# Hand-overs between the stages of an eight-stage Flamingo block: fewer returning transfers, other setup order, and small moves in the routing

## The chip, the core and the metric

One core of a Trainium2 chip runs the whole program in one launch. The metric is the device time in microseconds, median of repeated runs. TensorE multiplies and transposes (a transpose is a matmul with the identity), VectorE, ScalarE and GpSimd compute, and SP (SyncE) issues most transfers. Every stage is a block of its own: at its end all five engines meet, and GpSimd collects them and lets them go.

## The reference

`x` is 16 batches of 112 tokens of width 256, float32. Four layers follow, each a gated attention over a context of 375 tokens and a gated feed-forward net:

```python
x = x + tanh(g_xattn[l]) * xattn_l(layernorm(x), ctx)
x = x + tanh(g_ffn[l])   * ffn_l(layernorm(x))
# attention: softmax(q k^T * scale + mask) v, then an output projection and bias
#   layer 0: 8 heads of 32, then a spline (KAN) layer;   layer 1: 16 heads of 64, key mask
#   layer 2: 16 heads of 16, rotary q and k;             layer 3: 16 heads of 16, score mask
# nets: 0: soft decision tree;  1: 8 experts, dense, top-2 gates
#   2: 8 experts, rms norm, top-2 softmax, silu(x W1a + b) * (x W1b + b) W2
#   3: 9 experts, sigmoid scores, top-2, silu(x w1) * (x w3) w2
```

## The kernel before

`x_all` [112 tokens, 16 batches, 256] stays in SBUF between stages. An attention stage is a software pipeline over batches b = -1 .. 16: at step t the engines work at batch t's probabilities and prepare batch t+1 (norm, transposes, q, k, v). Four groups of four heads (i = 0 .. 3) make up a step; `CYCLES` says which projection TensorE does between the transposes of a group. Each engine's program is written out in order, and semaphores tie them:

- VectorE: `begin_norm` (bn_stats, bn_aggr, variance + eps; line 1011 ff.), then GpSimd's `power` (line 532) gives 1/sqrt, then VectorE's `norm_apply` (line 1022) writes `xn`. TensorE turns `xn` (line 670), ScalarE copies it, and q is projected. In layers 2 and 3 q is then split in two halves (`halve_q`, line 1080); in layer 2 GpSimd first rotates k (lines 545 to 551) and q (559 to 567). The scores are at line 749, their row maximum at 1092 or 1098, the exponentials (ScalarE) at 869, the transposes of the probabilities at 762, their copies at 1118 (VectorE) and 876 (ScalarE), the product with v at 780.
- In the group loop VectorE begins the norm of batch t+2 in group i = 2 and applies that of t+1 in group 0.
- Setup at the start of a stage, on VectorE: clear `v` (layers 2 and 3, line 989) or the probabilities (layer 1, line 1007), turn the mask into summands (992), prepare the value bias (1000), which TensorE multiplies by the output weights (804) and VectorE adds to the bias row (1002, 1004). Only then comes `begin_norm(0)`. GpSimd first clears the semaphores of the stage before (`clear_spent`, line 127).

The routed stages (layers 2 and 3) normalise all rows (`kept`, 1993), turn them in eight pairs (1798), score them (1807), and choose two experts per token. A table in four rounds of eight columns then puts each token into a slot of 35 or 36 tiles of 128: per round VectorE marks the tile (`spots`, 2084), multiplies by the token's number (2087) and marks the slot (2089), GpSimd multiplies the marks by the token's share (1712), and TensorE sums (1842). The tiles follow: GpSimd gathers rows (1719), TensorE turns them (1856), up projections (1867), down (1878), VectorE scales (2123), GpSimd adds the rows to `sums` in HBM (1731). SP loads the weights of each tile, double buffered (1758 to 1765). At the end of layer 2's stage SP waits for the last add and brings x back, one transfer per batch (1778), all on one semaphore; the attention of layer 3 waits for batch b with `16 * (b + 1)`.

## Time and profile before

| | |
|---|---|
| median of 3 runs | 2823.93 us (2821.07 to 2824.85) |
| profiled execution | 2821.64 us, span 2819.8 us, mean granted clock 0.975 |
| busy TensorE / VectorE / ScalarE / GpSimd | 94% / 54% / 46% / 22% |
| HBM traffic | 250.08 MB read, 18.48 MB written |

The stages in the span, and TensorE's busy time in each:

| stage | us from the span's start | length | TensorE busy |
|---|---|---|---|
| layer 0 attention | 11 to 422 | 411 | 371.6 |
| layer 0 tree | 422 to 471 | 49 | 39.1 |
| layer 1 attention | 471 to 1205 | 734 | 720.6 |
| layer 1 experts, dense | 1205 to 1333 | 128 | 118.9 |
| layer 2 attention | 1333 to 1685 | 352 | 328.6 |
| layer 2 experts, routed | 1685 to 2125 | 440 | 410.6 |
| layer 3 attention | 2125 to 2469.7 | 344.7 | 325.4 |
| layer 3 experts, routed | 2469.7 to 2820 | 350.3 | 322.5 |

How to read it: what a stage's TensorE time leaves is idle time of the engine that does most. It is not spread evenly: it sits at the starts of the stages, in the routing, and in small repeated waits. A row of the timeline gives the start, the duration, the engine and line, what is written from what, and in brackets how long the engine stood idle before it and which engine ended that.

### The profile page before, as it was taken

Reading aid. Unit: us, or ns where it says so; the run is one execution under the profiler, and the core shown is the slowest. Engines: PE = TensorE matmul, PEld = TensorE weight load, DVE = VectorE, ACT = ScalarE, POOL = GpSimd, SP = SyncE. Lnnn points to the kernel's source line nnn. Section 1 sums busy time; section 2 is a strip of 40 time slices with the busy share of each in tenths; the row PEclk is TensorE's granted clock in tenths of the full one; section 3 lists DMA queues with packets and bytes.
Section 4 is the critical chain, followed back from the end, with each engine's and each line's share of the span. In section 5 each row is a group of like instructions: output and inputs, shape, how many; then the busy total and the mean of one; then the engine's idle time right before and its main releaser. Section 6 shows DMA issues by size and latency. Waiting matters only on the chain. (4 is left out here: it accounts for less than half of the span.)

```text
span 2819.8 us, 56614 instructions
## 1 busy us (share of the span) xinstructions
PE 2637.1 (94%) x19850; PEld 1993.0 (71%) x19850; DVE 1532.3 (54%) x4127; ACT 1285.7 (46%) x3546; POOL 622.8 (22%) x577
## 2 busy tenths in 40 slices
PE   6999978999999999889899988999997999979998
PEld 4777755666666666655666666999995777758887
DVE  4667757555555555446677774232325777752222
ACT  4777733343343434321676752333335777622221
POOL 1666551000000000010444331222220000023232
PEclk9999989999999999999999998999998999989999
DMA  4000002000000000010000016999981000059897
GB/s 123 18 18 18 12 10 99 13 13 7 13 7 13 8 12 7 1 34 3 18 24 18 18 34 219 327 330 328 329 282 50 18 22 20 7 193 310 306 305 239
DMA packets 92163, 269.52 MB, mean 96 GB/s; under 512 B 25276, under 2 KB 51124, under 8 KB 77588
## 3 DMA queue, kind: packets, MB, share of 16 engines
q1 hardware_dynamic: 74708, 244.48, 25.0%
q0 software_dynamic: 13632, 18.62, 3.1%
q10 hardware_dynamic: 3616, 3.67, 0.4%
q8 instruction: 129, 2.11, 0.3%
q14 instruction: 78, 0.64, 0.1%
HBM read 250.08 MB, written 18.48 MB: 95 GB/s over the span
## 5 line engine op out<-in xcount | busy, mean ns | idle before, releaser
L762 PEld LDWEIGHTS a_full_ps<-ident,a_probs 112*125 112x125 f32 x2688 | 368.1, 190 | 130.5 <-issue 65.2
L1867 PEld LDWEIGHTS m_banks<-m_x_inT,m_w 128*128 128x128 f32 x3824 | 437.0, 193 | 15.4 <-issue 13.6
L1867 PE MATMUL m_banks<-m_x_inT,m_w 128*128 128x128 f32 x3824 | 444.1, 277 | 1.4 <-ACT m_x_inT L1931 0.9
L762 PE MATMUL a_full_ps<-ident,a_probs 112*125 112x112 f32 x2688 | 418.3, 282 | 19.1 <-ACT a_v L838 7.0
L869 ACT ACTIVATE a_probs<-a_masked,a_negmax 112x375 f32<-112x375 f32 x512 | 305.5, 598 | 280.2 <-DVE a_negmax L1092 280.1
L1118 DVE COPY a_pT<-a_full_ps 125x448 f32<-125x448 f32 x448 | 276.5, 620 | 254.6 <-PE a_full_ps L762 251.4
L663 PE MATMUL a_full_ps<-attention_room 128*125 128x256 f32 (+1 forms) x960 | 329.8, 472 | 11.4 <-ACT a_qT L861 3.9
L655 PE MATMUL a_full_ps<-attention_room 128*128 128x375 f32 x896 | 322.4, 488 | 1.4 <-ACT a_q_raw L857 0.7
L1092 DVE CUSTOM_DVE_ANT_0 a_masked<-a_sc_ps,a_mask_add 112x375 f32<-112x375 f32 x512 | 249.6, 544 | 29.9 <-PE a_sc_ps L749 29.9
L780 PEld LDWEIGHTS a_o_ps<-a_pT,a_v 125*32 125x32 f32 (+1 forms) x5376 | 164.4, 118 | 134.2 <-issue 106.1
L869 ACT ACTIVATE a_probs<-a_sc_ps,a_negmax 112x375 f32<-112x375 f32 x384 | 216.6, 576 | 92.8 <-DVE a_negmax L1098 92.8
L749 PE MATMUL a_sc_ps<-a_kT,a_qT 32*112 32x375 f32 (+1 forms) x1792 | 241.2, 512 | 6.7 <-ACT a_probs L869 3.3
L1878 PE MATMUL m_banks<-m_w,m_hid 128*128 128x256 f32 x992 | 232.9, 383 | 0.0
L663 PEld LDWEIGHTS a_full_ps<-attention_room 128*125 128x125 f32 x960 | 166.0, 188 | 92.3 <-issue 65.4
L780 PE MATMUL a_o_ps<-a_pT,a_v 125*32 125x112 f32 (+1 forms) x5376 | 216.4, 266 | 14.4 <-DVE a_pT L1118 10.8
L1098 DVE TENSOR_REDUCE a_negmax<-a_sc_ps 112x2 f32<-112x750 f32 x192 | 171.3, 934 | 94.8 <-PE a_sc_ps L749 94.8
L1731 POOL DMA_INDIRECT p_sums<-m_y_out,m_put x71 | 112.6, 1586 | 479.6 <-DVE m_y_out L2123 285.7
L1945 ACT ACTIVATE m_silu<-m_banks,m_b 128x128 f32<-128x128 f32 x280 | 102.8, 367 | 240.3 <-PE m_banks L1867 232.7
L655 PEld LDWEIGHTS a_full_ps<-attention_room 128*128 128x128 f32 x896 | 159.9, 194 | 70.9 <-issue 3.4
L1878 PEld LDWEIGHTS m_banks<-m_w,m_hid 128*128 128x128 f32 x992 | 180.0, 190 | 31.9 <-issue 11.9
L532 POOL TENSOR_TENSOR a_rstd<-a_rstd,minus_half 112x1 f32<-112x1 f32 x64 | 35.2, 549 | 734.0 <-DVE a_rstd L1015 726.9
L2109 DVE SCALAR_TENSOR_TENSOR m_hid<-m_banks,m_b,m_silu 128x128 f32<-128x128 f32 x280 | 98.1, 351 | 163.2 <-ACT m_silu L1945 163.2
(261 smaller groups left out, 3449.0 us busy)
## 6 DMA issues: line engine op xcount, KB each, us to landing
m_w<-in_L2f_w SPq DMA_DIRECT2D x105, 1024.0 KB, 6.7
m_w<-in_L3f_w SPq DMA_DIRECT2D x72, 768.0 KB, 4.6
attention_room<-in_ctxT SPq DMA_DIRECT2D x64, 375.0 KB, 3.1
m_w<-in_L3f_w SPq DMA_DIRECT2D x36, 640.0 KB, 5.4
m_b<-in_L2f_b SPq DMA_DIRECT2D x35, 128.0 KB, 8.0
p_sums<-x_all ACTq DMA_DIRECT2D x2, 1792.0 KB, 8.8
p_rows<-m_kept SPq DMA_DIRECT2D x16, 224.0 KB, 3.5
attention_room<-in_L0x_spline_wT SPq DMA_DIRECT2D x1, 2048.0 KB, 10.9
```

Of the source, the lines that this page charges most:

```text
L655: mm = pe.matmul(use_ps[:, 0:SK], wk[:, c, u[1] * P:(u[1] + 1) * P], ctxT[:, par, c, :], start=(c == 0), stop=(c == DC - 1))
L663: mm = pe.matmul(use_ps[0:KT, 0:v_width], ctxT[:, par, c, k * KT:(k + 1) * KT], wv[:, c, part * v_width:(part + 1) * v_width], start=(c == ...
L749: pe.matmul(sc_ps[:, a, 0:SK], lhs, kT[r:r + k, par, c, :], start=True, stop=True)\
L762: mm = pe.transpose(full_ps[0:KT, bank_of["turn", i, k], (j % 4) * S:(j % 4 + 1) * S], probs[:, i % 2, a, t * KT:(t + 1) * KT], ident[0:S, ...
L780: mm = pe.matmul(o_ps[a % WIDE * VW:(a % WIDE + 1) * VW, block * S:(block + 1) * S], v[:, par, t, head(i, a), :], pT[:, i % 2, KC * a + t, :],
L869: act.activation(probs[:, i % 2, a, 0:SK], src, ACT.Exp, bias=negmax[:, m:m + 1], scale=-1.0 if mask else 1.0, accum_out=rowsum[:, par, n: ...
L1092: dve.tensor_tensor_reduce(out=masked[:, i % 2, a, :], in0=sc_ps[:, a, 0:SK], in1=bias, scale=-1.0, scalar=FLT_MAX, op0=ALU.add, op1=ALU.m ...
L1098: dve.tensor_reduce(negmax[:, m:m + 2], sc_ps[:, 2 * a:2 * a + 2, 0:SK], AX.X, ALU.max, negate=True).then_inc(s_max.sem, 1)
L1118: dve.tensor_copy(pT[:, i % 2, 4 * k:4 * (k + 1), :], full_ps[0:KT, bank_of["turn", i, k], 0:4 * S] .rearrange("p (j s) -> p j s", j=4)).t ...
L1731: pool.indirect_dma_start(plan.sums, bass.IndirectOffsetOnAxis(plan.put[:, t:t + 1], 0), y_out[:, t % 2, :], None, compute_op=ALU.add).the ...
L1867: mm = pe.matmul(ab_ps[:, (par * FC + f) % RING, i * SLOTS:(i + 1) * SLOTS], w[:, par, c, f * P:(f + 1) * P], x_inT[:, c, :], start=(c == ...
L1878: mm = pe.matmul(y_ps[:, par, 0:D], hid[parts[f], f, :], w2[parts[f], par, f, :], start=(f == 0), stop=(f == FC - 1))
```

## The change

Borders. (1) x comes back in five transfers (batches 0, 1, 2-3, 4-7, 8-15), each on a semaphore of its own, instead of sixteen. (2) GpSimd no longer waits for the last added rows itself; SP still does.

Attention setup. (3) `begin_norm(0)` is the first work of VectorE but for a small copy. (4) `v` is cleared by GpSimd, one half (1536 elements per partition) in step -1 and one in step 0, each behind or ahead of other work of that engine; ScalarE waits for the half that it writes. (5) The value bias, the score mask, and in layer 1 the bias scaling and the clearing of the probabilities move into step -1. (6) The semaphore clears move to the end of GpSimd's step -1, behind the bias add of batch 0.

Layer 3's loop. (7) The norm of batch t+1 is begun in group 0 of step t (before: t+2 in group 2) and applied in the same group, behind one copy; GpSimd's power leads its step.

Routing. (8) The first two groups of rows are normalised ahead of the memsets and the gate scale, and TensorE turns five pairs before it waits for the routing weights. (9) The multiplication by the shares goes from GpSimd (4 instructions of 8 columns) to ScalarE (32 of one column). (10) SP waits for the first two gathers before it issues the second tile's weights.

```diff
@@ attention_stage @@
+    normed = 1 if layer == 3 else 2
 # gpsimd
-                core.clear_spent(pool)
+                if kan:
+                    core.clear_spent(pool)
                 def body(t, par):
+                    if layer == 3 and exists(t + 1):
+                        power(t + 1)
+                    if hd == 16 and isinstance(t, int) and t < 1:
+                        pool.memset(v[:, t + 1], 0.0).then_inc(s_zero.sem, 1)
                     if rope and exists(t + 1):
                         rope_add(t + 1, 1 - par, 0)
-                    if exists(t + 1):
-                        if isinstance(t, int) and t == -1:
-                            pool.wait_ge(s_bo.sem, 3 if late else 1)
+                    if exists(t) and exists(t + 1):
                         add_bias(t + 1)
 ...
-                    if exists(t + 2):
+                    if exists(t + 2) and layer != 3:
                         power(t + 2)
 ...
+                    if isinstance(t, int) and t == -1:
+                        pool.wait_ge(s_bo.sem, 3 if late else 1)
+                        add_bias(0)
+                        core.clear_spent(pool)
 # scalar, copy of v
-                            act.wait_ge(s_zero.sem, 1)
+                            act.wait_ge(s_zero.sem, b + 1)
 # vector
-                if hd == 16:
-                    dve.memset(v[:], 0.0).then_inc(s_zero.sem, 1)
 ...
-                        if divided and i == 0 and exists(t + 1):
+                        if layer == 2 and i == 0 and exists(t + 1):
                             norm_apply(t + 1)
 ...
-                        if i == 2 and exists(t + 2):
-                            begin_norm(t + 2)
+                        if i == (0 if layer == 3 else 2) and exists(t + normed):
+                            begin_norm(t + normed)
 ...
-                            if not divided:
+                            if layer != 2:
                                 norm_apply(t + 1)
 ...
+                        if divided and isinstance(t, int) and t == -1 and i == 1:
+                            value_bias()
@@ moe_stage @@
+BACK = (range(0, 1), range(1, 2), range(2, 4), range(4, 8), range(8, B))
 # gpsimd
-                for p in range(C // SPOTS):
-                    c = slice(p * SPOTS, (p + 1) * SPOTS)
-                    pool.wait_ge(s_in_tile.sem, p + 1)
-                    pool.tensor_tensor(in_tile[:, c, SHARES:], spots[:, c], share ... ALU.mult)
-                pool.wait_ge(s_put.sem, 16 * T)
 # sync
                 def body(t, par):
+                    if isinstance(t, int) and t == 1:
+                        for i in range(2):
+                            sp.wait_ge(s_x[i].sem, 16)
                     load(t, par)
 ...
-                    for b in range(B):
-                        sp.dma_start(x_all[:, b, :], plan.sums[b * S:(b + 1) * S, :]).then_inc(s_back.sem, 16)
+                    for group, back in zip(BACK, s_back):
+                        sp.dma_start(x_all[:, group.start:group.stop, :], plan.sums[...]).then_inc(back.sem, 16)
 # tensor
+                for p in range(5):
+                    turn_pair(p)
                 pe.wait_ge(s_w.sem, 16 * len(loads))
 # scalar
+                for c in range(C):
+                    if c % SPOTS == 0:
+                        act.wait_ge(s_in_tile.sem, c // SPOTS + 1)
+                    ins = act.activation(in_tile[:, c, SHARES:], spots[:, c], ACT.Copy, scale=share[...][:, c:c + 1])
+                    if c % SPOTS == SPOTS - 1:
+                        ins.then_inc(s_shares.sem, 1)
```

VectorE at the start of layer 3's attention, before (a_bvb is the value bias spread over the tokens, a_qT the halved q):

```order
L989 MEMSET a_v 125x3072
L992 TENSOR_SCALAR a_mask_add<-a_mask_in 112x375
L1000 COPY a_bvb<-attention_room 128x224
L1002 TENSOR_TENSOR attention_room<-a_o_ps,attention_room 112x256
L1004 TENSOR_SCALAR attention_room<-attention_room,gates 112x256
L1011 BN_STATS a_stats<-x_all 112x6
L1013 BN_AGGR a_mv<-a_stats 112x2
L1015 TENSOR_SCALAR a_rstd<-a_mv 112x1
L1022 TENSOR_SCALAR a_xn<-x_all,a_mv,a_rstd 112x256
L1080 TENSOR_SCALAR a_qT<-a_qfull,attention_room 128x224 x2
```

and of the change (line numbers are the changed kernel's):

```order
L1007 COPY a_bvb<-attention_room 128x224
L1017 BN_STATS a_stats<-x_all 112x6
L1019 BN_AGGR a_mv<-a_stats 112x2
L1021 TENSOR_SCALAR a_rstd<-a_mv 112x1
L1028 TENSOR_SCALAR a_xn<-x_all,a_mv,a_rstd 112x256
L1012 TENSOR_TENSOR attention_room<-a_o_ps,attention_room 112x256
L1014 TENSOR_SCALAR attention_room<-attention_room,gates 112x256
L1291 TENSOR_SCALAR a_mask_add<-a_mask_in 112x375
L1086 TENSOR_SCALAR a_qT<-a_qfull,attention_room 128x224 x2
```

The clearing is gone from VectorE, and the bias row and the mask stand between xn and the halves of q. Layer 2's start is the same without the mask, and with the shuffles of k and q ahead of the bias row.

VectorE in one step of layer 3's loop, before: first group 2, then, after the row maxima, group 0 of the next step:

```order
L1080 TENSOR_SCALAR a_qT<-a_qfull,attention_room 128x224 x2
L1011 BN_STATS a_stats<-x_all 112x6
L1013 BN_AGGR a_mv<-a_stats 112x2
L1015 TENSOR_SCALAR a_rstd<-a_mv 112x1
L1118 COPY a_pT<-a_full_ps 125x448 x2
...
L1022 TENSOR_SCALAR a_xn<-x_all,a_mv,a_rstd 112x256
L1127 TENSOR_TENSOR a_oT<-a_o_ps,a_rt 128x224
L1118 COPY a_pT<-a_full_ps 125x448 x2
```

and of the change, group 0 and then group 2 of one step:

```order
L1133 TENSOR_TENSOR a_oT<-a_o_ps,a_rt 128x224
L1017 BN_STATS a_stats<-x_all 112x6
L1019 BN_AGGR a_mv<-a_stats 112x2
L1021 TENSOR_SCALAR a_rstd<-a_mv 112x1
L1124 COPY a_pT<-a_full_ps 125x448
L1028 TENSOR_SCALAR a_xn<-x_all,a_mv,a_rstd 112x256
L1124 COPY a_pT<-a_full_ps 125x448
...
L1086 TENSOR_SCALAR a_qT<-a_qfull,attention_room 128x224 x2
L1124 COPY a_pT<-a_full_ps 125x448 x2
```

The three statistics instructions left the place between q's halves and the two copies, and xn stands behind them and one copy of group 0.

GpSimd at the start of layer 3's attention, before (L127 clears a semaphore, L532 is the power, L538 the bias add):

```order
L127 ISA x45
L532 TENSOR_TENSOR a_rstd<-a_rstd,minus_half 112x1
L538 TENSOR_TENSOR x_all<-x_all,attention_room 112x256
L532 TENSOR_TENSOR a_rstd<-a_rstd,minus_half 112x1
L538 TENSOR_TENSOR x_all<-x_all,attention_room 112x256
```

and of the change:

```order
L535 TENSOR_TENSOR a_rstd<-a_rstd,minus_half 112x1
L619 MEMSET a_v 125x1536
L541 TENSOR_TENSOR x_all<-x_all,attention_room 112x256
L127 ISA x45
L535 TENSOR_TENSOR a_rstd<-a_rstd,minus_half 112x1
L619 MEMSET a_v 125x1536
L541 TENSOR_TENSOR x_all<-x_all,attention_room 112x256
```

The clears went behind the first bias add, and each power is followed by half of the clearing of v in the first two rounds.

## Rows read from the trace of the kernel before

**Rows 1.** Stretches: us, busy PE, PEld, DVE, ACT, POOL, PEclk, DMA, GB/s

```profile
1685.00:2125.00 440.00, 410.56 (x3028) 384.57 (x3028) 145.42 (x446) 141.40 (x398) 97.30 (x78) 0.96 0.89 299
```

**Rows 2.** Timeline, TensorE, layer 1's attention: start us, us, instruction, idle before

```profile
482.08 1.53 PE L655 MATMUL a_full_ps<-attention_room 128*128 128x375 f32 x4 [0.59 <-DVE a_v L1048]
```

**Rows 3.** Timeline, start of layer 2's attention, VectorE, ScalarE, GpSimd

```profile
1332.06 2.62 DVE L989 MEMSET a_v<- 125x3072 f32 x1 [0.99 <-PEq L2182]
...
1339.33 0.41 DVE L1022 TENSOR_SCALAR a_xn<-x_all,a_mv,a_rstd 112x256 f32<-112x256 f32 x1 [0.66 <-POOL a_rstd L532]
...
1341.90 0.60 ACT L857 ACTIVATE a_q_raw<-a_full_ps,attention_room 128x112 f32<-128x112 f32 x2 [1.30 <-PE a_full_ps L678]
...
1343.08 0.64 POOL L538 TENSOR_TENSOR x_all<-x_all,attention_room 112x256 f32<-112x256 f32 x1
...
1344.97 0.66 POOL L567 TENSOR_TENSOR a_qfull<-a_qrot_a,a_qrot_b 128x224 f32<-128x224 f32 x1 [0.18 <-POOL a_qrot_b L562]
```

**Rows 4.** Line 1993's instructions, ns min/median/max, and GpSimd's memset, routing of layer 2

```profile
L1993 DVE TENSOR_SCALAR m_kept<-x_all,m_mv,m_rstd x16: 394/402/1162, 1687.7 to 1693.3; 112x256 f32<-112x256 f32 x16
...
1689.17 0.89 POOL L1707 MEMSET attention_room<- 112x928 f32 x1
```

**Rows 5.** Timeline, table of layer 2, second round: VectorE, GpSimd; ScalarE later

```profile
1712.09 0.44 DVE L2084 TENSOR_TENSOR attention_room<-route_room,m_high 112x280 f32<-112x280 f32 x1
...
1712.67 0.95 DVE L2087 TENSOR_TENSOR attention_room<-attention_room,route_room 112x280 f32<-112x280 f32 x1
...
1713.54 1.21 DVE L2089 TENSOR_TENSOR net_room<-route_room,m_low 112x1024 f32<-112x1024 f32 x1
...
1712.66 0.65 POOL L1712 TENSOR_TENSOR attention_room<-attention_room,m_share 112x280 f32<-112x280 f32 x1 [1.94 <-DVEq L2086]
...
1722.72 0.20 ACT L1924 ACTIVATE m_part<-m_banks 128x35 f32<-128x35 f32 x1 [19.55 <-PE m_banks L1847]
```

**Rows 6.** Timeline, first gather and tiles, GpSimd, TensorE, layers 2 and 3

```profile
1723.81 1.24 POOL L1719 DMA_INDIRECT m_x_in<-p_rows,m_take  x1 [5.31 <-DVE m_take L2095]
...
1730.23 0.69 PE L1856 MATMUL m_banks<-ident,m_x_in 128*128 128x128 f32 x2 [3.93 <-DMA m_x_in<-p_rows,m_take]
...
1731.78 9.28 PE L1867 MATMUL m_banks<-m_x_inT,m_w 128*128 128x128 f32 x64 [0.87 <-ACT m_x_inT L1931]
...
1744.57 7.31 PE L1867 MATMUL m_banks<-m_x_inT,m_w 128*128 128x128 f32 x64
...
2511.30 1.10 POOL L1719 DMA_INDIRECT m_x_in<-p_rows,m_take  x1 [5.28 <-DVE m_take L2095]
...
2514.20 0.44 PE L1856 MATMUL m_banks<-ident,m_x_in 128*128 128x128 f32 x2 [0.36 <-DMA m_x_in<-p_rows,m_take]
```

**Rows 7.** Timeline, border to layer 3's attention: SP, VectorE, TensorE

```profile
2116.82 7.38 SPq L1778 DMA_DIRECT2D x_all<-p_sums  x16
...
2125.31 2.62 DVE L989 MEMSET a_v<- 125x3072 f32 x1 [12.45 <-PEq L1702]
...
2128.59 2.02 PE L804 MATMUL a_o_ps<-attention_room,a_bvb 128*112 128x256 f32 x4 [16.25 <-DVE a_bvb L1000]
...
2137.30 0.90 PE L749 MATMUL a_sc_ps<-a_kT,a_qT 32*112 32x375 f32 x8
```

**Rows 8.** Waits (total, times, longest us) and timeline inside layer 3's attention

```profile
PE a_o_ps L780 <- DVE a_pT L1118: 8.1, 14, 0.6
...
2317.94 0.42 DVE L1011 BATCH_NORM_STATS2 a_stats<-x_all 112x6 f32<-112x256 f32 x1
...
2318.96 0.55 POOL L532 TENSOR_TENSOR a_rstd<-a_rstd,minus_half 112x1 f32<-112x1 f32 x1 [10.49 <-DVE a_rstd L1015]
...
2327.56 0.08 DVE L1092 DVE_READ_ACCUMULATOR2_ANT a_negmax<- 112x1 f32 x1
...
2329.69 0.35 PE L670 MATMUL a_full_ps<-ident,a_xn 112*128 112x112 f32 x2
```

**Rows 9.** Timeline, GpSimd, start of the tree stage

```profile
421.81 3.27 POOL L109 TENSOR_TENSOR f_rstd<-f_rstd,minus_half 112x2 f32<-112x2 f32 x2 [12.42 <-issue]
```

62 lines of the change are left out of this document (32 added, 30 removed).

## The prediction, made before the changed kernel ran

> **What bounds the kernel now.** I read the busy table first, then the stretches by stage, then each stage border in order of time. The busy table gives TensorE 94% of the span, so only TensorE's idle time can be won. In the stretches that idle time lies at the borders, in the routing ahead of the expert tiles (29.4 us idle in the 440 of layer 2's expert stage, [rows 1]), and as one short stall per batch in the last attention stage [rows 8]. Inside the expert tiles TensorE stands back to back, though the DMA engines are 89% busy there [rows 1]; that matters for a rival. So each border is a chain, and a step's price is how much earlier the first matmul behind it can start.
>
> **Part 1, layer 1's attention start.** VectorE scaled the bias and cleared the probabilities before its first statistics and copies. TensorE stood idle 0.59 us ahead of the first key projection, for VectorE's last value copy [rows 2]. The clearing is not gone: it now stands behind the copies of the first group of heads, so it delays the next two copies instead. I take that idle, **0.6**, as won; bounds nothing (the clearing still in the way) and twice that (an earlier wait of the same kind goes too).
>
> **Part 2, layer 2's attention start.** Before, VectorE cleared the values (2.62 us), TensorE then did the value bias, and only then came the first statistics. From their start to xn's is 1.6 us (0.85 on VectorE, 0.24 to the power, 0.55 for it [rows 8]), so they began near 1337.7, 5.7 us after the clearing began at 1332.06 [rows 3]. Now only a small bias copy leads, so they begin near 1332.3. GpSimd's power then ends near 1333.9, but GpSimd next clears half of the values: 1536 elements at the rate of its 928 in 0.89 us [rows 4] is 1.5 us, to 1335.3. VectorE's xn works on the same SBUF side by side with it. In the routing the same kind of VectorE instruction took up to 1162 ns against 402 beside GpSimd's work [rows 4], so I let xn end behind the memset, at 1335.7, against 1339.74: 4.1 us earlier. From xn to q_raw took 2.76 us [rows 3], so q_raw is there at 1338.4. GpSimd's q rotation then began only at 1343.68, 1.2 behind q_raw, as the key rotation and the bias add (0.64) stood ahead; now the add stands at the end. I get qfull at 1340.5 instead of 1345.63: **5.1 us**. Bounds 4 (the key rotation late by a whole memset) and 6 (xn not held up).
> By the Trainium skill, page "SBUF — State Buffer", section on its ports ("Reading the diagram"), GpSimd and a VectorE operation in a two-port mode take one shared port pair as an exclusive lock for the whole instruction. That speaks against moving the memset to GpSimd right behind the power: by it xn waits out the memset, which is the 1.1 us I already counted from the rows; without it the start would gain 6.
>
> **The semaphore clears** also move to the end of GpSimd's first round. In the tree stage 41 of them stand ahead of the first power, which began at 421.81 with GpSimd waiting for nothing that the trace shows [rows 9], 3 us into the stage: some 70 ns each. Layer 2 clears 24 (1.7 us) and layer 3 45 (3.2 us), each before work that has 5 us of GpSimd idle ahead of it in the trace (layer 2) or starts later still (layer 3). Cost nothing; uncovered at most 3.
>
> **Part 3, routing, head (both expert stages).** The first two groups of rows are normalised before the memsets and the gate scale (about 0.9 us in layer 2, 0.6 in layer 3). But the fifth pair, which TensorE turns before the first scores, comes from the third group, and that is where it was. **0.2 and 0**, bounds 0 and 0.9.
>
> **Part 4, routing, table (both).** Each of four rounds on VectorE has three instructions; the second one, of the same 280 elements as the first, takes 0.95 us against 0.44, and starts within 0.01 us of GpSimd's multiply (0.65) [rows 5]. The change gives that multiply to ScalarE. Then the second should cost about 0.45: 4 x 0.5 = 2.0 us in each expert stage, since the table matmul of each round waits for VectorE. ScalarE has 8 instructions of 112x35 per round. One alone takes 0.20 [rows 5], so at most 1.6, and from the end of VectorE's first instruction to that of its third are 2.2 us now, 1.7 then [rows 5]; it just fits. Bounds: nothing (the 0.95 belongs to the shape), 2.1. I take **2.0 + 2.0**. The page named above says the same, of a GpSimd operation that reads SBUF and a VectorE one with two SBUF inputs; by it 4.0, by the shape alone 0. The trace agrees as far as the two rows go.
>
> **Part 5, the first rows in (both).** SP issued the weights of two tiles ahead of the first gather. In layer 2 the gather was issued at 1723.81 and its turn began at 1730.23: 6.4 us. In layer 3, with smaller weights almost landed, 2.9 [rows 6]. With tile 1's weights held back, layer 2 should see about 2.9: 3.5 us. TensorE then doesn't sit idle 3.93 us, and the first up projection (9.28 us against 7.31 for later tiles [rows 6]) should lose about 1 us. I take **4.5** for layer 2 (bounds 2.5 and 5.5) and **0.4** for layer 3 (0, 1).
>
> **Part 6, x back and layer 3's attention start.** Sixteen issues took 7.38 us on SP, 0.46 each; VectorE began 1.1 us behind the last [rows 7]. Five take 2.3: 5.1 us earlier. GpSimd's dropped wait is worth nothing by itself, as SP waits for the same transfers and all engines meet at the border. Inside the stage the statistics no longer stand behind the clearing (2.62 us) and the value bias. But TensorE begins cold with the key and value projections; at the rate of the value bias (2.02 us for four of 256 columns [rows 7]) they take 3.0 + 2.0 and end near 2125.1, so they, not xn (2123.8 behind the memset), are late next. The transposes then lie 8.4 us earlier than before, and the value bias in front of halving q takes back 1.5: first scores near 2130.3 instead of 2137.30 [rows 7]. Total 7.0, minus 0.4 for the second half's memset ahead of a value copy in round 0: **6.6**. Bounds 5 (SP's part alone) and 9.
>
> **Part 7, layer 3's loop.** TensorE waited 14 times, 0.58 us each, 8.1 in all, for VectorE's last copy before the fourth group, because the statistics (0.85) stood between [rows 8]. They move to the first group, and that stall goes. What is late next is xn: there VectorE does oT (0.33 apart), statistics 0.85, one copy, then waits for the power (issued 0.24 behind, 0.55 long [rows 8]). From the old start of xn, 2327.56, I get its new start at 2329.48 and its end at 2329.89, against the turn at 2329.69 [rows 8]: TensorE waits about 0.28. Sum: 14 x 0.58 - 15 x 0.28 = 8.1 - 4.2 = **3.9**. Bounds -1 (xn 0.6 late) and 8.
>
> **Sum:** 0.6 + 5.1 + 0.2 + 4.0 + 4.9 + 6.6 + 3.9 = 25.3 us. The profiled execution took 2821.64 (span 2819.8 and 1.8 around it), so 2796.3. The median of the three runs is 2.3 above it: **2798.5**.
>
> **Rivals.**
> *Loop rival.* xn reaches TensorE later than I stepped out, by 0.6 us per batch: the power held up on GpSimd, or VectorE's copies in the way. For it: power and xn have nothing between them but one copy. Against: GpSimd had been idle 10.49 us ahead of its power [rows 8], so nothing queues there. Price 15 x 0.6 = 9: 2807.5.
> *Borders rival.* Another wait is late at each start: the mask or context behind the returning x, cold TensorE, key rotation. Then parts 2, 5 and 6 give half, 8.3 less: 2807; with the loop at nothing too, 2811.
> *Table rival.* The 0.95 us is the shape, or ScalarE's eight instructions are longer than VectorE's pair. Parts 4 fall away: 2802.5. Against it stands the equal size of the first instruction.
> *Slower.* SP's new wait pushes tile 1's weights from 1713 to about 1728. At the stretch's mean of 299 GB/s [rows 1] one tile's weights (three transfers of 1024 KB and its biases, 3.3 MB) take 11 us, so they land about when I expect its up projection (1740). If they land late, TensorE waits, and with engines 89% busy no later tile wins the lead back. It decides from a landing 13 us or more behind need in both stages: 2798.5 + 4.9 + 26 = 2829. Against: the two up weights are issued first and are only 2 MB, 7 us.
>
> **How the numbers follow.** Chances: forecast 0.69 (own range 2791 to 2805), loop 0.12, borders 0.10, table 0.06, slower 0.03. The range of 8 in 10 is 2788 to 2811: the low ends of all bounds together would give 2813, the high ones 2788. A change under 0.2% (5.6 us) can't be told from none. Only the slower rival lies above, and a pile of low bounds reaches no change: faster 0.94, same 0.03, slower 0.03.
>
> **What would show it.** Right: VectorE's second table instruction near 0.45 us; no wait of TensorE for pT in the last attention stage, and a new one for xn of some 0.3 us; the first gather's turn 3 us behind its issue; 5 issues in 2.3 us; first scores 5 us (layer 2) and 7 us (layer 3) earlier from the end of the stage before. Wrong: waits of TensorE on expert weights, a wait for xn above 0.6 us, or stretches inside layers 0 and 1 that changed.

## The result and the profile after

The changed kernel takes 2803.61 us (median of 4 runs, 2801.02 to 2806.2). The kernel before, run beside it, takes 2822.5 (4 runs, 2819.93 to 2824.85). The ratio is 0.9935, 95% interval 0.9919 to 0.9951: 18.9 us faster, where 25.3 were forecast. The profiled execution of the changed kernel, 2806.2 us, is the slowest of its four.

To place the difference I took 64 marks that both traces have: VectorE's addition to `x_all` at the end of each attention batch (line 1134 before, 1140 after), 16 per layer. Between them lie the starts of the stages. The table compares stretches. The counting matmul is the first of line 1834 (1848 after), and the turned table is the start of the transposes of line 1847 (1861). "Others" is the range of the same stretch in the experiments' traces that kept that part as in the changed kernel, which tells what the one trace owes to chance.

| stretch (us) | before | after | others | gain | forecast |
|---|---|---|---|---|---|
| layer 0's last mark to layer 1's first | 142.92 | 143.61 | 143.56 to 143.60 | -0.7 | 0.6 |
| layer 1's last mark to layer 2's first | 178.77 | 174.74 | 174.1 to 175.4 | 4.0 | 5.1 |
| layer 2's last mark to the counting matmul | 18.95 | 21.02 | 19.8 to 21.0 | -2.1 | 0.2 |
| the same, layer 3 | 21.42 | 21.35 | 21.1 to 22.3 | 0.1 | 0 |
| counting to the turned table, both stages | 39.84 | 36.36 | 36.3 to 36.9 | 3.5 | 4.0 |
| turned table to the third tile's up projection, layer 2 | 32.96 | 27.88 | 27.4 to 28.2 | 5.1 | 4.5 |
| turned table to the fourth tile's up projection, layer 3 | 29.54 | 29.51 | 29.5 to 29.6 | 0.0 | 0.4 |
| SP's first issue of x back to layer 3's first scores | 20.48 | 13.80 | 13.3 to 13.9 | 6.7 | 7.0 |
| from there to layer 3's first mark | 32.48 | 32.93 | 32.9 | -0.45 | -0.4 |
| layer 3's marks 1 to 14 | 265.41 | 262.56 | 262.5 to 262.6 | 2.85 | 3.9 |

The gains make 19.0. The span fell by 15.4 only, and most of the rest is where the change edits nothing: layer 0 came 0.9 late, and the last batches of layers 1 and 2 took 1.3 and 1.7 longer, at a lower granted clock. Stretches with columns as in [rows 1], of before and then of after, at the end of layer 2's attention:

```profile
1673.00:1685.00 12.00, 7.70 (x112) 5.53 (x111) 6.04 (x12) 4.20 (x12) 0.40 (x1) 1.00 0.01 2
```

```profile
1673.00:1685.00 12.00, 8.90 (x102) 6.49 (x94) 5.40 (x11) 3.66 (x11) 0.40 (x1) 0.72 0.00 1
```

The third figure from the end is the clock: 1.00 (2.4 GHz) and then a mean of 0.72, for the same kind of work. Such places change from trace to trace by 1 to 3 us, and layer 0's first mark by up to 4, so single parts are judged by their own stretch, and by medians of five runs only from 3 us on. Not all of it need be chance. Layer 2's last batch took 10.9 us before, 12.6 to 13.1 in the changed kernel and in all ten experiments with a single edit, and 10.8 and 12.0 in the two with several. With one trace of the kernel before, it stays open whether the change costs some 1.7 us at that place.

Layer 1's start, TensorE, then ScalarE, answers to [rows 2]:

```profile
482.61 1.53 PE L665 MATMUL a_full_ps<-attention_room 128*128 128x375 f32 x4 [1.69 <-DVE a_v L1054]
...
491.35 1.28 ACT L883 ACT_TABLE_LOAD   x1 [1.11 <-DVE a_negmax L1098]
```

and of the kernel before, TensorE in the value projection, and ScalarE's load:

```profile
474.17 7.13 PE L663 MATMUL a_full_ps<-attention_room 128*125 128x512 f32 x16 [1.30 <-DVE a_v L1048]
...
489.72 1.28 ACT L869 ACT_TABLE_LOAD   x1
```

The key projection starts 14.05 us behind the start of the tree's last addition (14.52 before). The idle time right ahead of it did not go, it grew from 0.59 to 1.69 us, since the clearing of the probabilities now stands ahead of VectorE's last two value copies. What went is the earlier wait of 1.30 in the value projection. And the load of the exponential's table now waits for the first maximum; before, it ran ahead of it.

Layer 2's start, VectorE, TensorE, ScalarE, GpSimd, answers to [rows 3]:

```profile
1334.82 0.28 DVE L1007 COPY a_bvb<-attention_room 128x224 f32<-128x224 f32 x1 [0.32 <-PEq L2203]
...
1336.61 1.43 DVE L1028 TENSOR_SCALAR a_xn<-x_all,a_mv,a_rstd 112x256 f32<-112x256 f32 x1 [0.66 <-POOL a_rstd L535]
...
1339.27 2.02 PE L688 MATMUL a_full_ps<-a_xT,attention_room 128*128 128x112 f32 x8 [0.54 <-ACT a_xT L855]
...
1341.32 0.60 ACT L869 ACTIVATE a_q_raw<-a_full_ps,attention_room 128x112 f32<-128x112 f32 x2 [2.20 <-PE a_full_ps L688]
...
1336.52 1.37 POOL L619 MEMSET a_v<- 125x1536 f32 x1
...
1343.44 0.66 POOL L570 TENSOR_TENSOR a_qfull<-a_qrot_a,a_qrot_b 128x224 f32<-128x224 f32 x1 [0.18 <-POOL a_qrot_b L565]
```

xn takes 1.43 us for 0.41 and ends 0.15 behind GpSimd's clearing. The q projection takes 2.02 us, at the lower clock. In the kernel before, where TensorE had worked for 4.5 us without a break ahead of the turn of xn, it took 1.12:

```profile
1340.75 1.12 PE L678 MATMUL a_full_ps<-a_xT,attention_room 128*128 128x112 f32 x8 [0.54 <-ACT a_xT L843]
```

The table, VectorE's second instruction in the first round and then the second round, answers to [rows 5], and the first gather, to [rows 6]:

```profile
1713.06 0.45 DVE L2108 TENSOR_TENSOR attention_room<-attention_room,route_room 112x280 f32<-112x280 f32 x1 [0.50 <-DVE attention_room L2105]
...
1715.15 0.45 DVE L2108 TENSOR_TENSOR attention_room<-attention_room,route_room 112x280 f32<-112x280 f32 x1
...
1715.09 1.83 ACT L1940 ACTIVATE attention_room<-attention_room,m_share 112x35 f32<-112x35 f32 x8 [0.62 <-DVEq L2107]
...
1716.97 6.17 PE L1856 MATMUL m_banks<-net_room,attention_room 112*99 112x128 f32 x48 [0.22 <-ACT attention_room L1940]
...
1724.92 1.23 POOL L1730 DMA_INDIRECT m_x_in<-p_rows,m_take  x1 [34.16 <-DVE m_take L2116]
...
1727.92 0.44 PE L1870 MATMUL m_banks<-ident,m_x_in 128*128 128x128 f32 x2 [0.51 <-DMA m_x_in<-p_rows,m_take]
...
1729.22 7.38 PE L1881 MATMUL m_banks<-m_x_inT,m_w 128*128 128x128 f32 x64 [0.87 <-ACT m_x_inT L1952]
...
1743.19 1.14 ACT L1966 ACTIVATE m_silu<-m_banks,m_b 128x128 f32<-128x128 f32 x4 [5.27 <-DMA m_b<-in_L2f_b]
```

VectorE's instruction is 0.45, and TensorE's last three rounds stand in one piece. ScalarE's 1.83 per round still hides in the 2.09 of VectorE's. In layer 2 the first round has a pause of 0.50 us ahead of VectorE's second instruction, where the later rounds have 0.15. It stands in the changed kernel's trace and in all twelve of the experiments, also with the shares back on GpSimd, and not in layer 3; its cause stays open. The turn comes 3.0 us behind the gather (6.4 before). The last row is a new wait: the second tile's biases are issued behind 3 MB of weights.

The border to layer 3, SP, VectorE, TensorE, answers to [rows 7]:

```profile
2112.87 2.31 SPq L1791 DMA_DIRECT2D x_all<-p_sums  x5
...
2116.77 0.28 DVE L1007 COPY a_bvb<-attention_room 128x224 f32<-128x224 f32 x1 [7.88 <-PEq L1720]
...
2118.61 1.45 DVE L1028 TENSOR_SCALAR a_xn<-x_all,a_mv,a_rstd 112x256 f32<-112x256 f32 x1 [0.70 <-POOL a_rstd L535]
...
2126.67 0.90 PE L759 MATMUL a_sc_ps<-a_kT,a_qT 32*112 32x375 f32 x8 [1.35 <-DVE a_qT L1086]
```

Five issues in 2.31 us as forecast; but VectorE starts 1.59 behind the last one, where it was 1.11. And the loop of layer 3, waits (total, times, longest) and then two of TensorE's rows, answers to [rows 8]:

```profile
PE a_full_ps L680 <- DVE a_xn L1028: 3.2, 15, 0.7
```

```profile
2316.90 0.59 PE L772 MATMUL a_full_ps<-ident,a_probs 112*125 112x112 f32 x4
2317.77 0.38 PE L680 MATMUL a_full_ps<-ident,a_xn 112*128 112x112 f32 x2 [0.29 <-DVE a_xn L1028]
```

No wait for the copies is left, and a small new one for xn. It shows as 0.29, but the turn starts 0.87 behind the start of the transposes ahead of it, where before (2329.26 and 2329.69) it was 0.43.

### The profile page after: what moved, and what is told of

The parts are those of the page before. It is cut to its first block and busy times, and to the rows that moved or that the text cites. A ratio compares the mean times of both kernels' runs of the same rounds, so it can differ in the third digit from the quotient of the medians.

```text
span 2804.4 us, 56661 instructions
## 1 busy us (share of the span) xinstructions
PE 2645.1 (94%) x19850; PEld 1995.5 (71%) x19850; DVE 1529.1 (55%) x4125; ACT 1301.5 (46%) x3610; POOL 623.3 (22%) x573
## 5 line engine op out<-in xcount | busy, mean ns | idle before, releaser
L1881 PEld LDWEIGHTS m_banks<-m_x_inT,m_w 128*128 128x128 f32 x3824 | 435.2, 192 | 15.6 <-issue 13.9
L1892 PEld LDWEIGHTS m_banks<-m_w,m_hid 128*128 128x128 f32 x992 | 179.9, 190 | 32.0 <-issue 11.9
```

What stands on the lines that cost most here:

```text
L1881: mm = pe.matmul(ab_ps[:, (par * FC + f) % RING, i * SLOTS:(i + 1) * SLOTS], w[:, par, c, f * P:(f + 1) * P], x_inT[:, c, :], start=(c == ...
L1892: mm = pe.matmul(y_ps[:, par, 0:D], hid[parts[f], f, :], w2[parts[f], par, f, :], start=(f == 0), stop=(f == FC - 1))
```

## The experiments

All but the last two are the changed kernel (2803.6) with one edit. The last two put several together.

**Sixteen transfers** (`x_back16`).

```diff
-sp.dma_start(x_all[:, group...], ...).then_inc(back.sem, 16)
+for b in group:
+    sp.dma_start(x_all[:, b, :], plan.sums[b*S:(b+1)*S, :]).then_inc(back.sem, 16)
```

> The changed kernel with x back in sixteen transfers, each group of batches still on its own semaphore. Forecast's theory (the number of issues sets the start of layer 3): SP's issues take 7.4 us for 2.3, the end of the last issue lies 5.1 later, the first scores of layer 3 at least 4 later after SP's first issue (13.8 us in the changed kernel), and the median rises from 2803.6 to about 2808. Rival (the transfers' landing and something else at the border set it, since 1.55 us pass between the last of the five issues and the release of the engines, where it was 0.39): then that gap shrinks to about 0.4 again, the start is only 4 us later, and the median is about 2807.5. If the issues are nothing at all: 2803.6.

Measured: 2808.3 (2806.52 to 2810.35), 4.7 more. SP issues from 2112.53 for 7.38 us, and VectorE's first row:

```profile
2120.34 0.28 DVE L1007 COPY a_bvb<-attention_room 128x224 f32<-128x224 f32 x1 [11.71 <-PEq L1720]
```

That is 0.43 behind the last issue. From the first issue to the first scores 17.71 us pass, 13.80 with five. So five transfers are worth 3.9 at the border and not 5.1, and something else takes the last 1.2 (the next experiment tells what).

**GpSimd's last wait back** (`x_poolwait`).

```diff
 for t in range(T):
     ...
     add(t)
+pool.wait_ge(s_put.sem, 16 * T)
```

> The changed kernel with GpSimd's last wait for the added rows put back. The forecast put its removal at nothing, since SP waits for the same transfers. Theory A (the 1.55 us between the end of SP's last issue and the release come from SP, whose last transfer is eight batches long): gap stays 1.55, time stays 2803.6 within 1 us. Rival B (GpSimd is now the last at the border): the gap changes by more than 0.3 us, growing if GpSimd's end starts only behind the wait, time up to 2 us longer, since both routed stages have the wait.

Measured: 2805.34 (2804.19 to 2810.75). SP, then VectorE:

```profile
2110.72 2.31 SPq L1792 DMA_DIRECT2D x_all<-p_sums  x5
...
2116.94 0.28 DVE L1007 COPY a_bvb<-attention_room 128x224 f32<-128x224 f32 x1 [10.31 <-PEq L1720]
```

The gap behind the last issue is 3.91 now, and the start comes 6.22 behind SP's first issue, where it is 3.90 without the wait. The rival holds: GpSimd is last at the border. It needs some 6 us from its last work to the meeting, whether that is the issue of the last add (2109.16 + 1.55 to 2116.77) or the end of its wait (2110.72 to 2116.94). A later experiment (the first clearing ahead of the power) has a row of GpSimd right behind the border, which names its own queue as what ended 6.03 us of idle time:

```profile
2115.81 1.38 POOL L638 MEMSET a_v<- 125x1536 f32 x1 [6.03 <-POOLq L1722]
```

What its queue runs in that time is a DRAIN at the stage's end; what that waits for the trace doesn't show. Min, median and max in ns of the two routed stages, with the start of the first and of the last, in the kernel before and in the changed one:

```profile
L1702 POOLq DRAIN  x2: 5773/5851/5929, 2117.0 to 2811.8; - x2
```

```profile
L1720 POOLq DRAIN  x2: 7565/7646/7726, 2108.9 to 2792.6; - x2
```

In layer 2's stage it ended at 2122.8 before, ahead of SP's last issue (2124.2), and at 2116.5 in the changed kernel, behind SP's (2115.2), 0.3 ahead of VectorE's start. Before, then, SP's 7.4 us covered it. The engines' release, the moment at which GpSimd lets them go, comes 7.7 us behind SP's first issue with sixteen transfers, with GpSimd's wait (before) and without it (x_back16). With five, it comes 3.8 behind without and 6.1 with the wait. So the removed wait is worth nothing alone and 2.3 us once the transfers are few. VectorE's start gained 0.7 more than the release: the clearing, which came first before, began 0.8 behind the release (2124.5 to 2125.31), the copy that comes first now 0.1 behind it.

**Layer 3's loop as before** (`loop_old`).

```diff
-if i == (0 if layer == 3 else 2) and exists(t + normed): begin_norm(t + normed)
+if i == 2 and exists(t + 2): begin_norm(t + 2)      # apply ahead of oT, power(t + 2)
```

> The changed kernel with layer 3's loop as before: statistics of batch t+2 in the third group, normalisation ahead of oT. Theory from the two traces: the wait of TensorE for the probabilities' copy comes back (14 times 0.58 us), the wait for xn (14 times, 2.6 us in all) goes, and the batches are 0.22 us longer each: 2803.6 + 2.9 = 2806.5. The forecast's own sizes say 3.9 longer, 2807.5. Rival (the loop gives nothing, the difference between the traces is the start of the stage): 2803.6 and a constant distance from batch to batch. The start loses nothing, as the first statistics still come first.

Measured: 2809.88 (2805.5 to 2811.51). The waits inside the loop:

```profile
PE a_o_ps L790 <- DVE a_pT L1124: 8.0, 14, 0.6
```

The marks of layer 3 keep their distance to those of the kernel before to 0.01 us over thirteen batches. So the whole gain of 0.22 to 0.23 per batch, 2.85, is this edit. The median moved more than that (6.3); this trace has layer 0's first mark 4.1 later than before, 3.5 later than the changed kernel's.

**Statistics in the fourth group** (`loop_g3`).

```diff
-    normed = 1 if layer == 3 else 2
+    normed = 2
-if i == (0 if layer == 3 else 2) and exists(t + normed): begin_norm(t + normed)
+if i == (3 if layer == 3 else 2) and exists(t + normed): begin_norm(t + normed)
```

> The changed kernel, but in layer 3 the statistics of batch t+2 stand in the fourth group, ahead of the copies, where VectorE was idle 0.82 and 0.68 us for TensorE; GpSimd's power stays first in its step. Theory (the xn wait is the chain statistics, power, xn inside one group; each wait costs its 0.2 to 0.3 us and the lost overlap of about 0.15 besides): both waits of TensorE are gone, each batch 0.4 us shorter, 14 x 0.4 = 5.6: 2798. Rival (the copies behind the statistics in the fourth group now come late, 0.85 less 0.82 idle and a semaphore): a new wait of TensorE for the probabilities' copy of some 0.2 to 0.5 us takes the place, 2801 to 2806.

Measured: 2798.6 (2795.68 to 2799.96), 5.0 less. Inside the loop only one wait of TensorE is left, once. VectorE's rows, in which the statistics fill what was idle time, and the copy starts at once behind them:

```profile
PE a_full_ps L688 <- ACT a_pT L890: 0.8, 1, 0.8
```

```profile
2247.88 0.37 DVE L1017 BATCH_NORM_STATS2 a_stats<-x_all 112x6 f32<-112x256 f32 x1
...
2248.79 0.62 DVE L1124 COPY a_pT<-a_full_ps 125x448 f32<-125x448 f32 x1
```

Each batch is now 0.58 shorter than before, the wait of [rows 8], and 0.36 shorter than in the changed kernel. So the wait for xn, which the trace shows with 0.2 on average, costs 0.36: a transpose that follows another at once starts 0.16 ahead of its modelled end (0.59 long, 0.43 apart), and a wait loses that too.

**The shares back on GpSimd** (`shares_pool`).

```diff
-act.activation(in_tile[:, c, SHARES:], spots[:, c], ACT.Copy, scale=share[...][:, c:c + 1])   # x32
+pool.tensor_tensor(in_tile[:, c, SHARES:], spots[:, c], share[...], ALU.mult)                 # x4
```

> The changed kernel with the multiplication by the shares back on GpSimd (4 instructions of eight columns). Forecast's theory (VectorE's second table instruction pays for running beside GpSimd's multiply): it takes 0.95 us again for 0.45, a round 2.6 us for 2.1, each table of layers 2 and 3 is 1.5 to 2.0 us longer, median 2803.6 + 3.5 = 2807. Rival (0.95 belonged to the other parts of the kernel before, or to the shape): 0.45 stays and the time is 2803.6.

Measured: 2807.16 (2802.43 to 2808.08). GpSimd and VectorE, second round:

```profile
1711.93 0.65 POOL L1730 TENSOR_TENSOR attention_room<-attention_room,m_share 112x280 f32<-112x280 f32 x1 [1.94 <-DVEq L2107]
1711.94 0.95 DVE L2108 TENSOR_TENSOR attention_room<-attention_room,route_room 112x280 f32<-112x280 f32 x1
```

0.95 comes back, and the tables are as long as before to 0.03 us (19.78 and 20.05 from the counting matmul, 18.25 and 18.11 in the changed kernel).

**Without SP's wait** (`sp_nowait`).

```diff
-if isinstance(t, int) and t == 1:
-    for i in range(2): sp.wait_ge(s_x[i].sem, 16)
```

> The changed kernel without SP's wait for the first two gathers. Forecast's theory (the weights of tile 1 delay the first rows): in layer 2 the first turn comes 6.4 us behind the gather's issue for 3.0, the first up projection takes about 9.3 us for 7.4, and from the end of the table to the third tile's up projection 33.3 us pass for 28.3: 2803.6 + 5 + 0.3 for layer 3 = 2809. ScalarE's wait of 5.3 us for the biases of tile 1 goes, and with it a stall of 0.47 that is in these 28.3. Rival (the wait only moves the loss, as the biases now come late): 2803.6 to 2805.

Measured: 2805.48 (2805.25 to 2806.46). TensorE's first turn and first up projection:

```profile
1729.98 0.69 PE L1867 MATMUL m_banks<-ident,m_x_in 128*128 128x128 f32 x2 [4.22 <-DMA m_x_in<-p_rows,m_take]
...
1731.53 9.13 PE L1878 MATMUL m_banks<-m_x_inT,m_w 128*128 128x128 f32 x64 [0.87 <-ACT m_x_inT L1949]
```

From the turned table to the third up projection 33.11 us, 5.2 more than in the changed kernel. The median, for which 2809 was expected, shows 1.9 of it. At layer 3's fifteenth mark this trace is 3.1 behind the changed kernel's, and the last batch, at the lower clock in the changed kernel's profile alone, makes them equal. So it is the stretch, not the median, that decides for the forecast's theory.

**Biases first** (`bias_first`).

```diff
+if biased and t < 2: biases(t, par, e)        # b1, b3 on s_bias_w, ahead of SP's wait
-    down_weights_in(act, t, par)              # ahead of the first silu
+    act.wait_ge(s_bias_w[par].sem, half(t, par) * 2)
```

> The changed kernel, where the two small bias transfers of tiles 0 and 1 of layer 2 are issued ahead of the weights and of SP's wait, on a semaphore of their own, so that ScalarE's silu waits for them and not for all 3 MB of the tile. Theory (the late biases cost the stall in tile 1's up projection): ScalarE's wait of 5.27 us goes, the up projection of tile 1 is one stretch of 7.3 us, and the third tile's begins 28.3 - 0.5 = 27.8 us after the end of the table: median 2803.1, less than a time can tell, so the trace decides. Rival (the weights of tile 1, issued at the same moment, are late as well): TensorE waits for them and 28.3 stays.

Measured: 2804.76 (2800.82 to 2806.95). The second tile's up projection is one piece:

```profile
1739.67 7.31 PE L1889 MATMUL m_banks<-m_x_inT,m_w 128*128 128x128 f32 x64
```

27.44 from the table to the third tile, 0.44 less. Three other traces with the late biases have 27.4 to 27.5 as well, and one has 28.2. In the nine traces with late biases (these, the changed kernel's and four more) the stall goes with ScalarE's wait for them: with waits of 3.93, 4.12 and 4.38 us the up projection takes 7.31 as here, and with 5.01 to 5.43 it takes 7.53 to 7.95, in the order of the waits. So it is the late biases that cost it, and only when they land late enough. The median, 1.2 above the changed kernel's, is no evidence either way.

**First clearing ahead of the power** (`v_first`).

```diff
+if hd == 16: pool.memset(v[:, 0], 0.0)        # ahead of power(0)
-if hd == 16 and t < 1: pool.memset(v[:, t + 1], 0.0)
+if hd == 16 and t == 0: pool.memset(v[:, t + 1], 0.0)
```

> The changed kernel with GpSimd's first clearing (1536 elements, 1.37 us) ahead of the first power instead of behind it, in layers 2 and 3, so that VectorE's xn has nothing beside it. Theory (xn took 1.43 and 1.45 us for 0.41 because GpSimd cleared v at that time): xn takes 0.41 in both. In layer 2 the start to the first scores (10.7 us in the changed kernel) is 1.0 shorter; in layer 3 TensorE's cold projections (v until 2121.5 in the changed kernel) are the later ones, and nothing is gained: 2802.6. Rival (xn was slow for another reason, as the first instruction with these operands): 1.4 us again, 2803.6. Second rival: the clearing slows the statistics instead, beside which it now runs, and the power starts up to 0.5 late.

Measured: 2801.36 (2799.36 to 2807.0). VectorE, layer 2:

```profile
1332.46 1.47 DVE L1009 COPY a_bvb<-attention_room 128x224 f32<-128x224 f32 x1 [0.32 <-PEq L2205]
...
1335.45 0.41 DVE L1030 TENSOR_SCALAR a_xn<-x_all,a_mv,a_rstd 112x256 f32<-112x256 f32 x1 [0.67 <-POOL a_rstd L535]
```

xn is back at 0.41, as the first theory had it, but the small copy that now stands beside the clearing takes 1.47 for 0.28. The loss moved and the start gained nothing: xn ends 3.40 us behind VectorE's first instruction, where it was 3.22. (The first scores come at 11.7 us, but without this edit they vary from 10.5 to 11.6.) That is the second rival, one instruction earlier than it said. What pays is the copy or TENSOR_SCALAR of VectorE that meets GpSimd's clearing, wherever that is put.

**Layer 1's wait moved** (`l1_act`).

```diff
-if b == 0 and i == 0 and which[0] == 0: act.wait_ge(s_zero.sem, 1)    # ahead of the first exponential
+if b == 0 and u[1] == 0: act.wait_ge(s_zero.sem, 1)                   # ahead of the first q copy
```

> The changed kernel, but in layer 1 ScalarE waits for the cleared probabilities ahead of its first q copy, not ahead of its first exponential. In seven traces with the change the first update of layer 1 comes 0.64 to 0.69 us later after the tree's than before, where the forecast put 0.6 less. Theory: with a second wait in front of the first exponential, the 1.28 us load of the exponential's table, which before ran while ScalarE waited for the first maximum, now starts behind it (491.35 for 489.72): 1.1 lost, and 0.5 gained at the first key projection. With the wait moved, the table load is hidden again, the distance from the tree's end to layer 1's first update is 1.1 us shorter: 142.5 for 143.6, median 2802.5. Rival (the loss is the clearing of the probabilities standing between VectorE's copies): 143.6 stays, 2803.6.

Measured: 2802.7 (2799.44 to 2804.11). ScalarE:

```profile
490.43 1.28 ACT L883 ACT_TABLE_LOAD   x1
```

The load waits for nothing. The stretch to layer 1's first mark is 142.47, 1.14 less than in the changed kernel and 0.45 less than before.

**Routing's head as before** (`head_old`).

```diff
-apply(0); apply(1); <memsets, gate scale>; apply(2)
+<memsets, gate scale>; apply(0); apply(1); apply(2)
-for p in range(5): turn_pair(p)  ...  pe.wait_ge(s_w ...)
+pe.wait_ge(s_w ...)  ...  for p in range(5): turn_pair(p)
```

> The changed kernel with the head of both routings as before: memsets and gate scale ahead of the rows, TensorE's wait for the weights ahead of its pairs. From the last update of layer 2 to the counting matmul were 18.95 us before and 19.8 to 21.0 in nine traces with the new head; in layer 3 21.4 and 21.1 to 22.3. The forecast: 0.2 gained in layer 2, nothing in layer 3, so 2803.8. Rival (the new head puts TensorE's turns apart, so that it runs at the lower clock when the scores come): about 19 us comes back in layer 2, and up to 1 us in layer 3, 2802. If it is the clock at the end of the stage before alone that differs, the distance stays at 20 or 21.

Measured: 2800.54 (2797.69 to 2805.43). TensorE in layer 2 of this kernel, then of the changed one:

```profile
1689.65 2.50 PE L1813 MATMUL m_banks<-ident,m_kept 112*128 112x112 f32 x12 [0.21 <-DVE m_kept L2007]
...
1694.43 0.93 PE L1813 MATMUL m_banks<-ident,m_kept 112*128 112x112 f32 x8
1696.05 0.96 PE L1822 MATMUL m_banks<-attention_room,route_room 128*32 128x224 f32 x16 [0.69 <-ACT attention_room L1911]
```

```profile
1690.96 1.01 PE L1813 MATMUL m_banks<-ident,m_kept 112*128 112x112 f32 x4 [0.20 <-DVE m_kept L2007]
1692.56 1.01 PE L1813 MATMUL m_banks<-ident,m_kept 112*128 112x112 f32 x4 [0.59 <-DVE m_kept L2007]
...
1696.38 1.70 PE L1813 MATMUL m_banks<-ident,m_kept 112*128 112x112 f32 x8
1698.71 1.72 PE L1822 MATMUL m_banks<-attention_room,route_room 128*32 128x224 f32 x16 [0.63 <-ACT attention_room L1911]
```

Layer 2's stretch to the counting matmul is 18.83 and layer 3's 21.05. The first scores begin 9.3 us behind layer 2's last mark in this kernel and 9.2 in the changed one, so the gaps of 0.20 and 0.59 in the turns delay nothing by themselves. The loss stands behind them: the last eight turns take 1.70 us for 0.93 and the second scores 1.72 for 0.96, at a granted clock of 0.50 over these rows (the lower level, 1.2 GHz) where this kernel has 1.00. The new head loses at least 1.0 us in layer 2 (19.8 to 21.0 in eleven traces that have it, 18.5 to 18.95 in the three that don't) and up to 1.3 in layer 3. It is the order inside the head that decides, and not the clock at the end of layer 2's attention: this kernel came out of that stage at a mean clock of 0.73 in the last 12 us and took 18.83, and the next version came out of it at 1.00 with the new head and took 21.02. That the gaps are what keeps the clock down is the likely reading; no run has the gaps alone.

**Six edits together** (`combo`): loop_g3, bias_first, l1_act, the clearing of layer 1's probabilities in group 2, the value bias and the mask behind the halving of q, and the first clearing of v behind xn (layer 3) and the first key rotation (layer 2).

```diff
-if divided and t == -1 and i == 1: value_bias()
+if divided and t == -1 and i == 2: value_bias()
+pool.wait_ge(s_xn.sem, s_xn.at(0)); pool.memset(v[:, 0], 0.0)     # behind rope_add(0, ...)
```

> A version with six edits on the changed kernel: layer 3's statistics of batch t+2 in the fourth group (measured 2798.6); the biases of the tiles in layer 2 on their own semaphore and first (the up projection of tile 1 without its stall, up to 0.5); GpSimd clears the first half of v behind xn (layer 3) and behind the first key rotation (layer 2), where VectorE has nothing that it could slow; VectorE finishes the value bias and the score mask in the third group, behind the halving of q; ScalarE's wait of layer 1 ahead of its q copy; the clearing of layer 1's probabilities in the third group, where VectorE is idle for 7 us. Theory: xn takes 0.41 us in both starts and the copy ahead of it 0.28; layer 2 starts 1.0 us sooner; layer 3 from the release of the engines to its first scores takes 8.7 us for 9.9 (0.4 + 0.4 + 0.35 of VectorE's work moved behind the halving); layer 1 1.1 + 0.5 less than in the changed kernel. 2798.6 - 0.3 - 1.0 - 1.2 - 1.6 = 2794.5. Rival (at these starts TensorE's projections at the lower clock are what is late, and VectorE's gains are covered by them): only the loop and layer 1 count, 2797.

Measured: 2799.03 (2796.52 to 2801.52), no better than the loop's edit alone. Layer 1's start gave 1.9, and layer 3 takes 8.48 us for 9.90 from VectorE's first instruction to the first scores, as expected. The theory had 2794.5 and missed by 4.5. Layer 2's first scores gained nothing (10.71 us behind VectorE's first instruction): GpSimd's q rotation, then TensorE's first scores:

```profile
1337.93 1.38 POOL L624 MEMSET a_v<- 125x1536 f32 x1
1339.27 0.58 POOL L562 TENSOR_TENSOR a_qrot_a<-a_q_raw,attention_room 128x224 f32<-128x224 f32 x1
...
1341.99 1.61 PE L762 MATMUL a_sc_ps<-a_kT,a_qT 32*112 32x375 f32 x8 [2.39 <-DVE a_qT L1089]
```

The clearing stood in front of the rotation, whose q was there at 1337.2. And behind the scores this start lost more. VectorE:

```profile
1343.60 1.64 DVE L1017 TENSOR_SCALAR attention_room<-attention_room,gates 112x256 f32<-112x256 f32 x1
1345.17 1.77 DVE L1107 TENSOR_REDUCE a_negmax<-a_sc_ps 112x2 f32<-112x750 f32 x2
```

The bias row, moved behind the halving, now stands ahead of the first row maximum, and its multiplication takes 1.64 us for 0.35 beside GpSimd's next key rotation. The maximum begins 13.9 us behind VectorE's first instruction (11.4 to 12.6 without the edits, 15.5 before), and layer 2's first mark comes at 48.6, against 44.8 to 47.1 without and 48.8 before: most of what part 2 had won is gone again. This is read from the traces; no run moved the bias row alone.

**Eight edits** (`combo2`): the same with head_old, and in both layers the clearing behind rope_q.

```diff
+if hd == 16 and t == -1: pool.wait_ge(s_xn.sem, s_xn.at(0)); pool.memset(v[:, 0], 0.0)   # behind rope_q(0)
```

> The version of six edits (2799.0) with the head of both routings as before (alone it took 19 us in place of 20 to 21 in layer 2, 21.05 for 22.3 in layer 3, median 2800.5 for 2803.6) and, in layer 2, GpSimd's first clearing behind the rotation of q; there it had stood ahead of it and held it up: the rotation began at 1339.27, just behind the clearing, and TensorE waited 2.39 us for the halved q. Theory: layer 2 from the release to its first scores takes 10.7 - 1.3 = 9.4 us, the two heads 1.2 each less: 2799.0 - 1.3 - 2.4 = 2795.3. Rival (the clock takes back what the starts give, as in the six-edit version, where the trace forecast 1.6 to 4 more than the median showed): 2797.5 to 2799. Second rival: ScalarE's first copy of v, which waits for the clearing, comes late and holds the exponentials: the first update of layer 2 is 1 us later though the scores are sooner.

Measured: 2792.68 (4 runs, 2792.02 to 2794.65), ratio to the kernel before 0.9893 (0.9876 to 0.9909). It beats both kernels, and the changed one by 10.9. That is 2.6 less than the theory's 2795.3. The heads take 18.52 and 21.07. Layer 2's start took only 0.3 less, since the clearing now runs beside the halving:

```profile
1343.02 1.65 DVE L1089 TENSOR_SCALAR a_qT<-a_qfull,attention_room 128x224 f32<-128x224 f32 x2 [1.63 <-POOL a_qfull L570]
```

It is 0.58 without a neighbour. The bias row still stands ahead of the row maximum, which begins at 13.6 us, and layer 2's first mark comes at 48.4: later than in the changed kernel though the scores are sooner, as the second rival said, but by the bias row and not by ScalarE's copy of v. In layer 3 the first scores come 7.90 us behind VectorE's first instruction (8.48 with six edits, 9.4 to 9.9 without). Which place gave more than the theory had is not known.

## Why the prediction was right, and where it was not

The time, 2803.6, lies in the range and inside the forecast's own 2791 to 2805, and none of the rivals is what happened as a whole. But the gain, 18.9, is three quarters of the 25.3, nearly all parts missed to the same side, and there is luck in the time: the kernel before, run beside the changed one, took 1.4 less than the 2823.93 from which I started. From 2823.93 the same gain gives 2805.0, the edge of that range. By its parts:

- *Part 1, failed, in two steps.* I took the idle 0.59 ahead of the first key projection as won. It grew to 1.69, since the clearing now stands in front of two copies (my lower bound), and what went is an earlier wait of 1.30 (my upper one); together the projection came 0.47 sooner. What I left out is that the new wait stands ahead of ScalarE's first exponential. I counted it at nothing and didn't ask what is behind the waiting instruction: a table load of 1.28 us. It costs 1.1, shown by l1_act.
- *Part 2, right in mechanism, 1.1 too large.* Statistics 0.2 behind the start and xn ending with the clearing went as stepped; xn ended 3.2 us behind the start for the 3.6 that I had. The mis-sized term is from xn to q_raw, for which I took 2.76 from [rows 3]; it measured 3.9, since the q projection now runs at the lower clock (2.02 for eight matmuls, 1.12 before). On the held-up xn I had gone by [rows 4] and by the Trainium skill, page "SBUF — State Buffer", section on its ports, which states an exclusive lock between GpSimd and VectorE's two-port modes. The trace agrees: 1.43 us beside a clearing of 1.37, 0.41 alone; v_first and combo2 move the loss to a copy (1.47) and to the halving (1.65).
- *Part 3, wrong sign.* I asked only when the fifth pair's input is there, and that step held: the first scores came less than 0.1 sooner. I didn't ask at which clock the work behind them runs. The trace lost 2.1 in layer 2; head_old shows at least 1.0 of it to be this edit, and 0 to 1.3 in layer 3.
- *Part 4, right.* 0.95 became 0.45, and shares_pool brings it back. 1.5 and 1.95 for 2.0 each. In layer 2 the pause in the first round (0.50 for 0.15) takes 0.35 of the missing 0.5. ScalarE's eight instructions take 1.83, not the 1.6 at most that one of 0.20 suggested, and end 0.2 behind VectorE's third, which can account for the last 0.1.
- *Part 5, right.* 5.1 for 4.5 in layer 2, nothing for 0.4 in layer 3. sp_nowait gives it back. The slower rival's mechanism (late second tile) showed in a small form: biases, not weights, nothing to 0.6 us.
- *Part 6, right in sum (6.2 for 6.6), wrong in one step.* I priced the border by SP alone and put GpSimd's dropped wait at nothing. That holds with sixteen transfers; with five it is worth 2.3, and even so GpSimd's DRAIN is last, so the release is 3.9 earlier and not 5.1. VectorE's start is 4.6 earlier, as its first work no longer is the clearing. The rest, cold projections first, value bias in front of the halving, went as stepped.
- *Part 7, right in mechanism, 2.85 for 3.9.* The stall is gone and xn is late by 0.2 to 0.3, as worked out. The mis-sized term is the price of that wait: 0.36 each, for the 0.28 that I took. With 0.36 my own sum, 14 and 15 terms, gives 2.7; the marks cover thirteen distances. loop_g3 shows it.

Together these miss 1.3 + 1.1 + 2.2 + 0.5 + 0.4 + 1.05, less 0.2 that part 5 gave beyond its term, 6.3: the distance from 25.3 to the 19 found in the stretches and 18.9 in the medians. If the 1.7 us at the end of layer 2's attention belong to the change, that match is in part chance. The "borders rival" had the right kind of loss (cold TensorE, another wait late at each start) for parts 2 and 6, at about a sixth of its size: parts 2, 5 and 6 together gave 1.3 less, where it had 8.3.

## What to carry to other kernels

When an instruction gets a second wait, look at what runs between the two, a table load above all, and put the new wait on an earlier instruction that has room. Work moved to GpSimd isn't free for VectorE while it runs, so place it where VectorE has nothing that meets it and where no rotation or power stands behind it. Work moved behind one link of a chain stands in front of the next one: step out that one as well, here the row maximum. Price a border by all the engines that meet there, not by the one that is last now.

## What the runs showed of the hardware

- A clearing of 1536 elements on GpSimd (1.37 us) held up VectorE's TENSOR_SCALAR of 256 elements (0.41 to 1.43), a copy of 224 (0.28 to 1.47) and a TENSOR_SCALAR pair (0.58 to 1.65), each until about its end (changed kernel, v_first, combo2); the row maximum of 375 elements beside one kept its 0.55 (layer 3 of the six-edit version). Two multiplications of the key rotation on GpSimd held a TENSOR_SCALAR of 256 elements from 0.35 to 1.64 (the six-edit version).
- GpSimd reached the meeting of the engines some 6 us behind its last indirect transfer, or behind its wait for it. Its queue's DRAIN took 5.77 us behind the wait and, begun ahead of the last transfer, 7.57 us without it.
- In layer 3's loop a wait of TensorE behind transposes cost about 0.15 us more than it shows (0.29 shown, 0.44 later; on average 0.21 shown, 0.36 per batch).
- With nothing changed in them, the ends of attention stages took 1 to 3.3 us more or less from trace to trace, at mean granted clocks of 0.60 to 1.00. The last batch of layer 3 took 15.16 us in the changed kernel's profile, at a mean of 0.70, and 11.9 at 1.00 in eight of the experiments.
